# Leaving the filler matmuls out of TensorE's plan in a two-layer decoder kernel

## What is computed

```python
x = x + _L0_attn_ref(_layernorm(x), ...)    # four 256x256 products, a = sigmoid, h[t] = a[t]*h[t-1] + d*b, out projection
x = x + _L0_xattn_ref(_layernorm(x), ctx, ctx, mask0, ...)          # cross attention, 16 heads of 16, 64 keys
x = x + _L0_ffn_ref(_layernorm(x), ...)                             # one 256x256 product (low-rank part folded in)
x = x + _L1_attn_ref(_layernorm(x), ...)    # LSTM of 20 units over time -> position weights -> weighted sum of earlier x
x = x + _L1_xattn_ref(_layernorm(x), ctx, ctx, fside, mask1, ...)   # cross attention with a gate on the weights
x = x + _L1_ffn_ref(_layernorm(x), ...)     # router, best of 8 experts, 256 -> 128 -> 256 each
```

## Time and profile before

| | before |
|---|---|
| median of 3 runs | 3078.72 us (3077.14 to 3085.44) |
| the profiled execution's own time | 3086.61 us |
| its span, first to last instruction | 3084.7 us |
| busy: PE / DVE / POOL / ACT | 88% / 66% / 34% / 30% |
| mean granted TensorE clock | 0.919 of full speed |
| fillers | 140 in stage 0, 1077 in stages 4 and 5 |

### The profile page before, as it was taken

One profiled execution on the slowest core, in us unless ns is written; L12 is line 12 of the kernel. 1 busy time (PEld: TensorE's weight loads), 2 busy tenths in 40 slices (PEclk: granted clock), 3 DMA queues, 4 the chain that ended last, 5 costly groups with the idle time before them and its releaser, 6 DMA issues.

```text
span 3084.7 us, 38068 instructions
## 1 busy us (share of the span) xinstructions
PE 2724.8 (88%) x11733; PEld 1591.8 (52%) x11733; DVE 2042.3 (66%) x6490; ACT 932.5 (30%) x2361; POOL 1045.9 (34%) x956
## 2 busy tenths in 40 slices
PE   5799897886888988897988889898999998999999
PEld 2465554352555555463645555554555554555555
DVE  3576776887878696867778696866475664434433
ACT  0133233242324233332423233332322332222222
POOL 0254432332525242513425242513141340422422
PEclk9899897897899899888888999998999998999999
DMA  5210201001010101101010101000011010110100
GB/s 173 68 50 14 64 1 50 1 28 60 15 52 15 53 14 39 35 12 48 26 48 14 59 14 38 22 27 28 29 34 34 14 35 28 42 41 16 53 27 8
DMA packets 127166, 110.37 MB, mean 36 GB/s; under 512 B 31234, under 2 KB 126039, under 8 KB 126624
## 3 DMA queue, kind: packets, MB, share of 16 engines
q1 hardware_dynamic: 127008, 108.55, 11.4%
HBM read 76.81 MB, written 31.72 MB: 35 GB/s over the span
## 4 chain that ended last, share of the span: by engine, by line
PE 40%; issue 26%; DVE 23%; POOL 8%; ACT 2%; SPq 1%; DMA 1%; POOLq 0%; DVEq 0%; ACTq 0%
PE p L687 4%; PE p L781 4%; PE p L842 4%; PE p L854 4%; PE p L744 4%; PE p L720 3%; DVE l_xnat L1049 3%; DVE uin L1278 3%; PE p L681 3%; PE p L698 3%; PE pg L753 2%; PE p L734 2%; POOL l_scratch L1360 2%; DVE ln_stats L1024 2%; DVE l_scratch L1075 2%
## 5 line engine op out<-in xcount | busy, mean ns | idle before, releaser
L1348 POOL TENSOR_TENSOR l_kbd<-l_kg,headmask 128x512 f32<-128x512 f32 x256 | 265.4, 1047 | 376.7 <-PE p L720 277.4
L1334 POOL TENSOR_TENSOR ln_rstd<-ln_ve,neghalf 128x4 f32<-128x4 f32 x96 | 97.9, 1020 | 863.5 <-DVE ln_ve L1033 862.9
L1278 DVE SCALAR_TENSOR_TENSOR uin<-gates 16x20 f32<-16x20 f32 x512 | 185.7, 363 | 215.2 <-ACT gates L879 212.3
L1355 POOL TENSOR_TENSOR l_scratch<-l_scratch,l_mx 128x512 f32<-128x512 f32 x256 | 266.7, 1046 | 148.7 <-DVE l_mx L1079 147.9
L744 PEld LDWEIGHTS p<-l_vg,l_scratch 128*128 128x128 f32 x2048 | 266.1, 202 | 95.8 <-DVE l_xnat L1092 37.9
L879 ACT ACTIVATE gates<-pg 16x80 f32<-16x80 f32 x512 | 115.2, 225 | 650.7 <-PE pg L753 649.5
L720 PE MATMUL p<-l_kbd,l_qT 128*128 128x512 f32 x512 | 282.9, 642 | 22.5 <-DVE l_scratch L1075 21.8
L744 PE MATMUL p<-l_vg,l_scratch 128*128 128x34 f32 x2048 | 278.2, 285 | 17.7 <-DVE l_xnat L1092 9.5
L761 PE MATMUL p<-warm 128*128 128x512 bf16 x1077 | 286.8, 395 | 0.0
L842 PE MATMUL p<-l_xT,wfc 128*128 128x512 f32 x512 | 283.4, 647 | 1.1 <-DVE hr L1232 1.0
L854 PE MATMUL p<-wpj,hq 128*128 128x256 f32 x1024 | 264.9, 387 | 8.5 <-ACT hq L955 8.5
(11 more groups left out here) (166 smaller groups left out, 4762.4 us busy)
## 6 DMA issues: line engine op xcount, KB each, us to landing
xln<-xln_dram SPq DMA_DIRECT2D x40, 512.0 KB, 3.9
l_vg<-v_dram SPq DMA_DIRECT2D x32, 544.0 KB, 3.9
l_kg<-k_dram SPq DMA_DIRECT2D x32, 256.0 KB, 4.2
xln_dram<-l_xnat SPq DMA_DIRECT2D x16, 512.0 KB, 3.0
x_dram<-l_xres SPq DMA_DIRECT2D x16, 512.0 KB, 4.1
l_xres<-x_dram SPq DMA_DIRECT2D x16, 512.0 KB, 3.7
out<-l_xres SPq DMA_DIRECT2D x16, 512.0 KB, 2.9
xin<-in_x SPq DMA_DIRECT2D x12, 512.0 KB, 3.8
```

Source lines behind the costliest of these rows:

```text
L1278: dve.scalar_tensor_tensor(uin[:, :], gates[:, 0:20], 1.0, gates[:, 60:80], ALU.add, ALU.mult)
L1348: pool.tensor_tensor(w.kbd[b % 2][:, j, :, :], w.kg[:, j, b:b + 1, :].broadcast_to([P, NE, SK]), headmask[:, :].rearrange("p (a o) -> p a ...
L1355: pool.tensor_tensor(ex, ex, w.mx[:, i_ % 4, :].rearrange("p (a o) -> p a o", o=1).broadcast_to([P, NE, SK]), ALU.subtract).then_inc(t.shi ...
```

## The change

The tuple of stages that get fillers is made empty. No filler is planned in any stage; the search that orders the real steps is the same and comes before the fillers are put in, so their order does not change. The waits, tiles and all other engines' instructions stay as they are; the tile `warm` is still filled once.

```diff
-IDLE, FILL, WARM = 0.3, 0.9, (0, 4, 5)
+IDLE, FILL, WARM = 0.3, 0.9, ()
```

## The result

| | before | changed |
|---|---|---|
| median | 3080.94 us (4 runs, 3077.14 to 3085.44) | 3198.78 us (4 runs, 3192.81 to 3204.27) |
| ratio, 95% interval | | 1.038 [1.036, 1.041] |
| the profiled execution's own time | 3086.61 us | 3199.01 us |
| mean granted TensorE clock | 0.919 | 0.852 |

118 us more by the medians, 112.4 by the profiled executions, against 58 forecast. The direction and the cause were right, and the price of a low microsecond nearly so; the amount was not: 3198.8 lies 62 us above the predicted time and 4 us above the range.

What follows compares the result with a forecast made beforehand. In stages 4 and 5 one chain leaves PE dense or one link, with POOL leading in attention; fillers keep the clock up. 70 us lost less 12 given back is +58 us, 3137 us predicted, range 3092 to 3195.

Steps and rivals of the forecast that it cites:

- Slower, by the clock: Stages 0, 4 and 5: without fillers TensorE's clock falls, 70 us lost, 12 given back, +58 us; chance 0.60.
- Time given back: Stages 4 and 5: fillers no longer hold up real PE instructions behind them, 12 us, bounds nothing to 35.
- Before the query: Norm's gap, eight bodies: PE idle, so turn and query begin at the low clock, 2.4 x 8 = 19 us lost.
- router to experts: Eight bodies: router, turn and the experts' start run at the low clock, 2.8 x 8 = 22 us lost.
- body starts: Body start and position weights, eight bodies: 0.5 x 8 = 4 us lost.
- stage 0: Two lanes fill each other, norms mostly partly covered, a gap between two bodies: 4.5 x 2 = 9 us lost.
- Attention and output projection: Eight bodies: POOL covers most; if the clock falls, projection and the turn before it are exposed, 2.0 x 8 = 16 us.
- The check by rates: Clock 0.83 in stages 4 and 5, 0.91 in stage 0: 290 more low us cost 58 to 122 us.
- The signs: Changed profile: PE busy down some 250 us, stages 4 and 5 clock 0.78 to 0.87, stage 5 bodies 5 to 10 us longer.
- The clock costs more: Rival, chance 0.22: low clock on the single chain's path nearly always, rate 0.42, +110 us, 3189 us.
- Little happens: Rival, chance 0.09: clock falls only while PE has nothing to do, 0 to +8 us, about 3083 us.
- faster: Rival, chance 0.07: real work holds the full clock and the 35 us of fillers on the chain come back, 3044 us.

Runs made afterwards that it cites:

- half the dose: Each gap filled to 0.45 in place of 0.9 in stages 0, 4 and 5, against the kernel before: 1.0197 [1.017, 1.023], +61 us.

## Why the prediction was right and wrong

- *Slower, by the clock.* Right. The clock falls at the places named in the forecast, and fillers of 16 columns do not save it.
- *Time given back, 12 us (0 to 35).* Not measured by itself. The nearest runs speak for its order: twice as many short fillers cost 8 us or nothing in the way, a third more wide ones some 19 us by the estimate above.
- *Before the query 19 us, router to experts 22, body starts 4, stage 0 9.* Measured 24, 23, 2 and 8. Their working, half speed for some us into dense work, holds: the query's stretch runs at 0.59, and from router to first expert the last body takes 6.72 us in place of 4.68, the 2.0 of the prediction. One reading was off: the turn has 8 instructions in the trace and not 16, for a transpose is one and not two; the term did not hang on it.
- *Attention and output projection, 16 us.* This is the step that failed: 63 us, and 54 with attention's fillers alone gone. The 23 at its last turn, projection and norm answer to the "1.9 us and more" a body; the 40 inside attention had next to nothing. Two sentences were wrong. "POOL covers most of it": the chain of waits named POOL for 18 us of a body, and I took that for the whole of attention, while in stage 5 its end is a round trip of PE and ACT, and in stage 4 POOL is still at work and is held up with the rest. And "PE's density rises, and the clock with it": PE is busy 14.0 of 18.0 us there and the clock stays low, at 0.52.
- *The check by rates.* The rate was nearly right. The forecast's 0.24 leaves out the 12 us given back, and with them it is 58 / 290 = 0.20; 0.25 was measured with whatever was given back in it, 0.27 at half the dose. The low time was not right: 258 us more expected in stages 4 and 5, 444 measured, 217 of it in attention and what follows it to the turn. I set the clock to 0.83, below stage 3's 0.89, with PE busy 0.66 in mind; it is 0.75 and 0.78. I think that a mean busy share hides how stages 4 and 5 split into dense experts and a sparse rest; no run was made for that.
- *The signs.* Bodies of stages 4 and 5 were to grow by 5 to 10 us, and over 14 was to mean that the path is PE's alone. They grew by 11.1 to 16.6, 14.0 on average, right at that mark. PE's busy time was to fall by some 250 us and fell by 115. Stage 0's clock (0.90 for 0.91) and stages 1 to 3 came as said.
- *The Trainium skill.* "TensorE: Matmul & The Clock Gate", section "Terms", gives half the throttled time as the penalty: 222 us for 444. Measured is half of that, 111.6 us, so the rows of stage 3 judged it rightly. The same page's section "What's actually happening" puts the ramp at under 1% of a typical kernel's span. This case's loss is 3.8%, with a clock that falls again in every body.
- *The rivals.* "The clock costs more", 3189 us, comes nearest in time, by the wrong reason: it had the rate at 0.42 and the low time as forecast. "Little happens" and "faster" fell. The range's end at 3195 was set by that rival's rate; a second end, for the low time, was missing. With the measured 444 low us at the measured 0.25, and stage 0's 8, the median of before comes to 3198; that is bookkeeping and no forecast.

## What to carry to other kernels

Cost a fall of the clock as low time times a rate, and bound both: the rate from bodies that differ in clock alone, the low time place by place, not from a stretch's mean busy share. The rate is of its place: it was 0.22 to 0.31 in these kernels' stages 4 and 5, and perhaps 0.09 where two lanes run. A stage led by another engine is not covered all through; follow PE's own rounds at its start and end before its matmuls are counted as hidden. Fillers that wait for nothing and stay within a planned gap cost little, and on one chain of work they are worth keeping in short gaps as much as in long ones.

## What the runs showed of the hardware

- The clock went low, and stayed low for 20 us, where PE waited at most 1.2 us at a time (from 2994.7 us on, through the rounds and the projection above).
- Twice as many matmuls of 32 weights and 16 columns in the fillers' places left the mean clock at 0.853, where no fillers give 0.852; fillers of 64 weights and 512 columns held the clock as well as those of 128, 0.922 against 0.919.
- Going from instructions of 128 weights to a bf16 filler of 64 and back held PE up by 0.10 and 0.11 us at the place shown. The kernel with all 1217 fillers narrow took 12 us more, not all of it for this reason.
- With the fillers gone, a stretch of attention at a clock of 1.00 took the time of before (18.46 us against 18.48), and rounds at 0.50 took 3.57 us in place of 2.29.
